# A decoder layer on one core: the first weight sweep takes its block sums from accumulating DMAs that GpSimd issues

## What is computed

```
x = layernorm(x + autocorrelation_attention(x))
x = layernorm(x + softmax(ctx @ x^T / 16 over the rows of ctx) applied to ctx)
x = layernorm(x + x @ W^T + moe_lora(x))        # W is 2048 x 2048
```

## Time and profile before

| | |
|---|---|
| median of 3 runs | 1943.51 us (1940.82 to 1945.38) |
| the profiled execution's own time | 1942.99 us |
| its span | 1940.8 us |
| TensorE busy | 1785.7 us, 92% of the span |
| VectorE, ScalarE, GpSimd busy | 1359.9, 791.5, 184.8 us |
| mean granted clock of TensorE | 0.975 of 2.4 GHz |
| DMA | 472.70 MB, mean 244 GB/s |

### The profile page before, as it was taken

How to read it: one execution, slowest core, us unless ns; L and a number is a source line. 1 busy time by engine, 2 the same in 40 slices (tenths; PEclk the granted TensorE clock), 3 DMA queues, 4 the chain that set the end, 5 groups by cost and what they waited for, 6 DMA issues and landing times. The chain is left out here.

```text
span 1940.8 us, 27023 instructions
## 1 busy us (share of the span) xinstructions
PE 1785.7 (92%) x10194; PEld 953.7 (49%) x10210; DVE 1359.9 (70%) x2602; ACT 791.5 (41%) x939; POOL 184.8 (10%) x367
## 2 busy tenths in 40 slices
PE   4899999999947869999999999998899999999997
PEld 3666666666623334454444454443344444444443
DVE  5888888888869666776657777798654655565453
ACT  5888888888835212222222221143231222123111
POOL 1212121212400000000000000000100010011000
PEclk9999999999978889999999999998999999999999
DMA  8999999999785699999999999946999889988983
GB/s 268 242 289 267 292 251 292 264 293 260 239 217 204 168 216 262 254 250 249 256 256 261 243 214 251 208 160 169 301 260 252 275 217 261 260 254 246 254 247 120
DMA packets 565451, 472.70 MB, mean 244 GB/s; under 512 B 498432, under 2 KB 502528, under 8 KB 544384
## 3 DMA queue, kind: packets, MB, share of 16 engines
q1 hardware_dynamic: 565312, 470.87, 88.7%
HBM read 237.51 MB, written 109.58 MB: 179 GB/s over the span
## 5 line engine op out<-in xcount | busy, mean ns | idle before, releaser
L1670 PE MATMUL bank_f<-w_hi_f,a_cols 128*128 128x512 f16 x3584 | 1094.6, 383 | 47.7 <-DVE w_lo_f L1407 33.4
L1670 PE MATMUL bank_f<-w_lo_f,a_cols 128*128 128x512 f16 x1792 | 686.6, 383 | 0.0
L1670 PEld LDWEIGHTS bank_f<-w_hi_f,a_cols 128*128 128x128 f16 x3584 | 353.4, 99 | 476.9 <-DVE w_lo_f L1407 37.2
L1266 ACT ACTIVATE rows_f<-xn_f 128x1024 f16<-128x1024 f32 x75 | 79.2, 1057 | 491.1 <-DMA xn_f<-x_scratch 340.3
L1670 PEld LDWEIGHTS bank_f<-w_lo_f,a_cols 128*128 128x128 f16 x1792 | 176.6, 99 | 206.7 <-issue 6.8
L1438 DVE SCALAR_TENSOR_TENSOR y_f<-bank_f,w_iscale_f,y_f 128x512 f32<-128x512 f32 x192 | 134.6, 743 | 169.2 <-PE bank_f L1670 168.9
L771 PE MATMUL ps_s_fast<-k_both_fast,a_cols 128*128 128x256 f16 x1536 | 170.4, 273 | 1.1 <-DVE lscale_fast L589 1.0
L1438 DVE SCALAR_TENSOR_TENSOR y_f<-bank_f,w_iscale,y_f 128x512 f32<-128x512 f32 x192 | 134.9, 745 | 40.7 <-PE bank_f L1670 34.1
L771 PEld LDWEIGHTS ps_s_fast<-k_both_fast,a_cols 128*128 128x128 f16 x1536 | 150.2, 98 | 18.7 <-issue 1.0
L1399 DVE TENSOR_TENSOR rows_f<-xn_f,rows_f 128x1024 f16<-128x1024 f32 x75 | 90.8, 1211 | 97.0 <-ACT rows_f L1266 96.8
L1399 DVE TENSOR_TENSOR rows_f<-sums_f,rows_f 128x1024 f16<-128x1024 f32 x60 | 73.3, 1221 | 112.0 <-ACT rows_f L1266 111.8
(11 more groups left out here) (227 smaller groups left out, 2186.9 us busy)
## 6 DMA issues: line engine op xcount, KB each, us to landing
xbuf_fast<-x SPq DMA_DIRECT2D x32, 1024.0 KB, 7.7
x_scratch<-x2buf_fast SPq DMA_DIRECT2D x32, 1024.0 KB, 6.9
y_f<-x_scratch SPq DMA_DIRECT2D x32, 1024.0 KB, 7.6
xn_f<-x_scratch SPq DMA_DIRECT2D x60, 512.0 KB, 4.9
kept_scratch<-a_cols SPq DMA_DIRECT2D x45, 512.0 KB, 3.3
xn<-x_scratch SPq DMA_DIRECT2D x45, 512.0 KB, 6.8
a_cols<-kept_scratch SPq DMA_DIRECT2D x45, 512.0 KB, 8.7
cbuf<-ctx_in SPq DMA_DIRECT2D x16, 1024.0 KB, 5.6
```

The source lines that it names most:

```text
L1266: nc.scalar.activation(rows[g % 2][:, 0], source(i), ACT.Copy).then_inc(a_hi, 1)
L1670: ins = nc.tensor.matmul(bank[i][:], a_cols[:, i, part + kk, :], ww[:, W_SLOT[i], kk, :], start=(kk == 0 and part == 0 and ww is w_hi), st ...
```

## The change

For units 1 to 7 the three sums are no longer made by VectorE. SP loads raw blocks 0, 2 and 0 of the unit from HBM into combined(u) (load_both, 512 KB and 256 KB). When both loads have landed, GpSimd issues two DMAs that add blocks 1, 3 and 3 from HBM onto them (512 KB and 256 KB). ScalarE waits for these (both_done) before the high part of the sums. Unit 0, and units 8 to 15, keep the instructions that they had. combined(u) is y[0] for units 0, 2, 4, 6 and x_rows[0] for 1, 3, 5, 7; load_both(u) waits until unit u-2's low part of the sums is done. The raw unit is still loaded whole, for the blocks 0 and 3 and the differences. In SP's order load_both(u) stands ahead of load_unit(u), with load_both(1) and load_both(2) after load_unit(1); the residual load moves from after unit 5's load to after unit 7's and waits for the sums' low part of unit 6, since its buffer y[0] holds sums until then. In the attention pass the semaphore f_loaded is merged into tables_loaded.

```diff
@@ attention_pass
-                        sp.dma_start(first_tile, x2_out[P:2 * P, :]).then_inc(f_loaded, 16)
+                        sp.dma_start(first_tile, x2_out[P:2 * P, :]).then_inc(tables_loaded, 16)
...
-                            pool.wait_ge(f_loaded, 16)
+                            pool.wait_ge(tables_loaded, 48)
...
-                            act.wait_ge(f_loaded, 16)
+                            act.wait_ge(tables_loaded, 48)
@@ feed_forward
+        def by_dma(u):
+            return 0 < u < HK
+
+        def sums_done(u, k):
+            return 4 * u - 2 * min(max(u - 1, 0), HK - 1) + k
+
         def combined(u):
-            whole = y[0][:].rearrange("p t c -> p (t c)") if u < 4 else x_rows[0][:]
+            whole = y[0][:].rearrange("p t c -> p (t c)") if u < HK and u % 2 == 0 else x_rows[0][:]
             return blocks(whole[:, 0:3 * BANK], 3)
@@ SP
+                def load_both(u):
+                    if u > 1:
+                        sp.wait_ge(w_lo_done, 3 * (u - 2) + 2)
+                    chunk = blocks(w_chunks[u], 4)
+                    sp.dma_start(combined(u)[:, 0:2], chunk[:, 0::2]).then_inc(both_loaded[u % 2], 16)
+                    sp.dma_start(combined(u)[:, 2], chunk[:, 0]).then_inc(both_loaded[u % 2], 16)
...
                         if s == 0:
-                            sp.wait_ge(w_lo_done, 3 * 4)
+                            sp.wait_ge(w_lo_done, 3 * 6 + 2)
...
                 load_unit(1)
+                load_both(1)
+                load_both(2)
                 load_unit(2)
+                load_both(3)
                 for b in (A22, A21):
                     load_block(1, b)
                 load_unit(3)
+                load_both(4)
                 load_b(0)
                 load_unit(4)
+                load_both(5)
                 load_unit(5)
-                load_residual(0)
+                load_both(6)
                 load_unit(6)
+                load_both(7)
                 keep(0, 4)
                 keep(0, 5)
                 load_unit(7)
+                load_residual(0)
@@ GpSimd, after the all-reduce of the router's squares
+                for u in range(1, HK):
+                    pool.wait_ge(both_loaded[u % 2], 32 * ((u + 1) // 2))
+                    chunk = blocks(w_chunks[u], 4)
+                    g.dma_start(combined(u)[:, 0:2], chunk[:, 1::2], accum_op=ALU.add).then_inc(both_done[u % 2], 16)
+                    g.dma_start(combined(u)[:, 2], chunk[:, 3], accum_op=ALU.add).then_inc(both_done[u % 2], 16)
@@ ScalarE, unit_high
-                    act.wait_ge(w_sum, 4 * u + 2)
+                    if by_dma(u):
+                        act.wait_ge(both_done[u % 2], 32 * ((u + 1) // 2))
+                    else:
+                        act.wait_ge(w_sum, sums_done(u, 2))
...
-                    act.wait_ge(w_sum, 4 * u + 4)
+                    act.wait_ge(w_sum, sums_done(u + 1, 0))
@@ VectorE, unit_low
-                    after(dve, w_lo_done, 3 * (u - 1) + 2)
-                    v.tensor_tensor(both[:, 0:2], raw[:, 0::2], raw[:, 1::2], ALU.add).then_inc(w_sum, 1)
-                    v.tensor_tensor(both[:, 2], raw[:, 0], raw[:, 3], ALU.add).then_inc(w_sum, 1)
-                    dve.wait_ge(w_sum, 4 * u + 1)
+                    if not by_dma(u):
+                        after(dve, w_lo_done, 3 * (u - 1) + 2)
+                        v.tensor_tensor(both[:, 0:2], raw[:, 0::2], raw[:, 1::2], ALU.add).then_inc(w_sum, 1)
+                        v.tensor_tensor(both[:, 2], raw[:, 0], raw[:, 3], ALU.add).then_inc(w_sum, 1)
+                        dve.wait_ge(w_sum, sums_done(u, 1))
```

More of the change, by code:

```diff
@@ L211, in attention_pass @@
         w_loaded, w_squared, w_summed = sem("w_loaded"), sem("w_squared"), sem("w_summed")
-        f_loaded, f_sum, f_hi, f_lo, f_turned = sem("f_loaded"), sem("f_sum"), sem("f_hi"), sem("f_lo"), sem("f_turned")
+        f_sum, f_hi, f_lo, f_turned = sem("f_sum"), sem("f_hi"), sem("f_lo"), sem("f_turned")
         mv1_ready, mean2_ready, ssq2_ready, mv1_free = sem("mv1_ready"), sem("mean2_ready"), sem("ssq2_ready"), sem("mv1_free")
@@ L340, in _ @@
                     sp.wait_ge(stored[0][r], 16 * (base + nb // 2))
-                sp.wait_ge(tables_loaded, 16 * 4)
+                sp.wait_ge(tables_loaded, 16 * 5)
                 sp.wait_ge(f_turned, 16 * NM)
@@ L986, in feed_forward @@
         y_stored, first_loaded, first_stored = [sem(f"y_stored{i}") for i in range(2)], sem("first_loaded"), sem("first_stored")
-        residual = sem("residual")
+        residual, both_loaded, both_done = sem("residual"), [sem(f"both_loaded{i}") for i in range(2)], [sem(f"both_done{i}") for i in range(2)]
         kept_stored, kept_loaded = sem("kept_stored"), [sem(f"kept_loaded{i}") for i in KEPT]
```

## The result

The kernel after takes **1965.03 us** in the median of 4 runs (1962.43 to 1967.27), the kernel before 1943.01 in 4 runs beside them (1940.82 to 1945.38). The ratio is 1.0111, with a 95% interval of 1.0099 to 1.0123: 22 us slower. 1953.5 was predicted, so the direction was right and the loss came out at 2.1 times the 10.5 us of the sum. The measured time lies in the range (1942 to 1975). The profiled execution took 1967.27 us with a span of 1965.4, 24.6 more than the span of before.

A forecast was written before the change was run, and what follows sets the result against it. VectorE was taken to bound the first sweep, TensorE the rest. With the DMA loop at 18.0 us per two units, unit 7 ends at 651.2 instead of 640.7: 1943.0 + 10.5 = 1953.5 us, range 1942 to 1975.

The forecast's parts named there:

- What is taken away: First sweep: VectorE loses seven pairs of sums of 1.74 us, 12.2 us; at most 10.4 us of it can be won.
- Where the chain begins: Unit 1's additions start after GpSimd's router all-reduce (584.18); its low part 2 to 4 ends at 596.0, before 586.8.
- GpSimd's two issues: Time for GpSimd to issue a unit's two accumulating DMAs: 1.2 us, bounds 0.7 and 3.
- Bytes doubled by the adding: Accumulating 768 KB also fetches the destination, so bytes count double: 1.57 MB, 7.2 us with fixed time and crossing.
- Rival 1: An accumulation in the sweep costs what a load costs: P = 15.2 us, no change, 1943 us; chance 0.19.
- P: Loop time of one sums buffer in the first sweep, serving two units: 6.2 + 1.2 + 7.2 + 3.4 = 18.0 us.
- the loads' term of P: SP's two loads of 768 KB per unit: 4.4 us alone plus 1.8 for crossing transfers, 6.2, bounds 4.4 and 8.
- the bytes agree: Check of the loop: two units move 6.8 MB, 16.1 us at 423 GB/s, against 18.0 us.
- odd chain: Sums of units 1, 3, 5, 7 in one buffer end the sweep last: unit 7 done at 651.2, before 640.7.
- Rival 3: Adding in the DMA engines or GpSimd's descriptors is slow: P from 22 to 28, about +26 to +50 us; chance 0.22.
- TensorE's clock: At the sweep's end TensorE has transposes and unit 6 from 643.4 to 649.8, so unit 7 starts warm, no clock lost.
- What moves: Transfers reordered in SP's queue stay hidden: blocks and rows of B by over 10 us, the residual by 6 us.

The follow-up runs named there:

- second quarter kernel: The changed kernel with only the first 128 of 512 columns both loaded as first operands and added by GpSimd: 1943.85 us, ratio 0.9997.
- the quarter adds: The changed kernel with GpSimd adding only the first 128 of each block's 512 columns, first operands loaded whole: 1955.49 us, ratio 1.0067.

## Why the prediction was right in direction and half in size

- *What is taken away* held: the sums are gone from VectorE for units 1 to 7, and its total fell by 11.6 us.
- *Where the chain begins* came out right by two misses that cancel. GpSimd was free of its all-reduce at 584.12, as in the trace of before and so 1.8 us early against the later start; and ScalarE started 10.3 us after that, where 8.4 were predicted. That was luck. The low part of unit 1's sums ended at 597.78, predicted 596.0 + 1.8.
- *GpSimd's two issues*: 1.2 us predicted; the second begins 0.7 us after the first (1.05 the first time) and both are over after 2.0. Inside the bounds 0.7 to 3.
- *Bytes doubled by the adding* held, at 5.7 against 2.9 us of engine time per MB. The prediction's reason, that the destination is fetched as well, was its author's estimate: the doubled time and the 1.86 times as many packets agree with it, and no trace shows the reads themselves.
- *Rival 1*, that an accumulation costs a load, falls with that. Its sum was wrong as well: the kernel with plain DMAs fulfils its premise and is still 15 us slower than before, with P from 18.3 to 25.2 and not 15.2. 512 KB landed after 5.6 us as a plain copy in that busy sweep, and after 8.7 when added in the kernel after.
- **The step that failed** is the loads' term of P, and with it the check "the bytes agree": "I add 1.8. Take 6.2". The loads took 9.7 us in the mean, up to 13.7. On the even buffer this term is 11.9 us of the miss (13.7 + 10.6 against 2 x 6.2), and the accumulation's, mis-sized in the same way, 4.2 us (8.7 + 12.3 against 2 x 8.4). I priced crossing transfers as small additions, 1.8 and 1.0, and the bytes at 423 GB/s, the best slices of a stretch with nothing but a stream. That the adding took the engines longer does not explain the loads: with plain DMAs they still took 9.3 us. What shows is what crosses them: unit 4's load took 13.7 us among raw unit 3, two blocks and B's rows, 9.0 with the blocks and B's rows moved away, and in the second quarter kernel, where three of the four loads took 3.1 to 3.2 us, it still took 8.5. As for the check of the bytes, with the prices read above two units need 2 x (1.05 + 0.79) MB x 2.9 + 1.57 MB x 5.7 = 19.6 us of engine time, already more than P = 18.0, before any block or row of B. The rows to see it were at hand: 288 GB/s at a share of 0.81 and 231 at 0.73 are, as an estimate, 356 and 316 GB/s for full engines, not 423. (2.9 us per MB is 347, which agrees, though the slices of the earlier trace rows had shown more.) So the term needed what crosses it, priced byte by byte, and the check needed the engines' time.
- The *odd chain* was said to end last; it was the **even** one. Unit 6's sums, not unit 7's, set the end: their low part ended at 655.11 (predicted 637.3 + 1.8), and unit 7 then ran as fast as VectorE could make it, to 667.4, 12.3 us later, where 13.9 lay between the two predicted ends. 10.5 + 11.9 + 4.2 - 1.6 = 25.0, against 24.9 measured. Which buffer lost was decided by what happened to cross: raw unit 3, the blocks, the rows of B and unit 3's adding all met the load of unit 4's sums.
- *Rival 3* foresaw P of 22 to 28 by slow adding or slow descriptors. The even loop lay there (25.8, 26.2) and the odd one below it (21.9, 19.9), but not for its reason: GpSimd's two issues took 2.0 us, and adding cost 2, not 4, times the bytes. Its fear for a late first use did not show: the first DMA came 0.3 us after the all-reduce began.
- *TensorE's clock*: unit 7 started at full clock, as predicted. The traces give the clock as a share of full speed; the prediction's 1.2 GHz is, as an estimate, the rate of columns at half of it. Before, unit 0's matmuls of 512 columns began 0.43 us apart (share 0.50 from 581.0 to 584.4), 1.2 columns per ns, and unit 1's 0.21 us apart (share 1.00 from 587.9 to 593.0), 2.4 per ns. In the kernel after, unit 6's first ones (661.08, after an idle time of 13.6 us with four short transposes behind it) began 0.43 us apart and unit 7's (667.66) 0.21.
- *What moves* cost nothing of its own: the residual was issued at 655.23, landed 6.4 us later, and the first update started at 667.93. B, blocks and kept operands were not waited for, but their bytes were part of the sweep's 79 us, where the prediction called them hidden.

## What to carry to other kernels

Before you move arithmetic into transfers, add up the DMA engines' time in that stretch: its price per MB is a window's share times its length, divided by its MB, and twice that here for bytes that are added onto a destination. If the sum is near the stretch's length, transfers in it become late, also those that the change does not touch: the raw units took 9.7 to 11.3 us here instead of 5.9. And price two DMAs in series on a buffer with everything that crosses each of them: here they cost the sweep 21 us even as plain copies. A third buffer took 11 us back, a quarter of the bytes in both steps 23.5, and neither made a kernel that beats the one before. Ask first what the relief is worth with its bytes in place: here 3 us of sweep for 12.2 us of VectorE.

## What was not expected of the hardware

- An accumulation from HBM into SBUF needs 5.7 us of all 16 engines per MB, 1.97 times what SP's queue needs beside it, and 1.86 times the packets of the same copy. In pieces of 512 bytes (the quarter adds) it is worse: 12.4% of 92 us for 1.38 MB is 8.3 us per MB.
- GpSimd's first elementwise add came 11.9 us after its all-reduce with nothing to wait for in the trace, while in the kernel after its first DMA issue came 0.3 us after the all-reduce began. What the 11.9 us are was not tried.
- A saturated stretch, part of it adding, moved 309 GB/s (share 1.05), not the 423 that a stream reached.
